# Graph network with residual norms: three buffers of dst rows, preloaded groups spread over the first pass, convolutions in halves

## What is computed

```python
N, E, D, H, L = 50000, 12500, 256, 8, 3       # nodes, edges sorted by dst, features, heads, layers
# 1. attention over the edges, relu, residual, layer norm over all nodes
h = x @ W;  e = leaky_relu(a_src[src] + a_dst[dst], 0.2)
alpha = exp(e - segment_max(e, dst)[dst]) / (segment_sum(...)[dst] + 1e-16)
x = layernorm(x + relu(segment_sum(h[src] * alpha, dst) + bias))
# 2. three edge convolutions, each followed by a batch norm; residual, layer norm
y = x
for l in range(3):
    e = relu((y[dst] - y[src]) @ theta[l].T + y[src] @ phi[l].T)
    agg = where(segment_max(e, src) < -1e30, 0, segment_max(e, src))
    y = relu((agg - agg.mean(0)) * rsqrt(agg.var(0) + 1e-5) * gamma[l] + beta[l])
return layernorm(x + y)
```

## Time and profile before

| | us |
|---|---|
| runs (three), median and extremes | 1758.32 (1757.24 to 1765.64) |
| the profiled execution, own time | 1768.92 |
| its span | 1767.1 |
| granted TensorE clock, mean of the span | 0.834 |
| PE busy | 1076.6 |
| DVE busy | 1239.4 |
| ACT busy | 985.7 |
| POOL busy | 955.6 |

### The profile page before, as it was taken

The page is one execution under the profiler, slowest core; times in us unless marked ns, Lnnn a source line. Parts: engine busy times, 40 slices in busy tenths (PEclk is TensorE's granted clock), DMA queues, the critical chain, the costliest instruction groups (busy, mean ns, idle before and its releaser), DMA issues.

```text
span 1767.1 us, 16600 instructions
## 1 busy us (share of the span) xinstructions
PE 1076.6 (61%) x3823; PEld 562.5 (32%) x3823; DVE 1239.4 (70%) x2657; ACT 985.7 (56%) x2630; POOL 955.6 (54%) x1013
## 2 busy tenths in 40 slices
PE   0139888781004661699999699997999987000000
PEld 0023333330002331455555355554545544000000
DVE  8847877678978994255455355563666678989998
ACT  4735877665455775244444455564555453766665
POOL 1047756667767777777777677524544137640000
PEclk9999999895557876799999899998999999555555
DMA  9276899988694674588886589856866359999999
GB/s 366 101 227 214 284 324 354 334 306 257 222 294 157 202 228 144 155 261 264 255 269 203 120 187 202 184 162 122 153 141 134 84 186 309 420 412 389 383 404 366
DMA packets 174965, 431.98 MB, mean 244 GB/s; under 512 B 28308, under 2 KB 107682, under 8 KB 154900
## 3 DMA queue, kind: packets, MB, share of 16 engines
q1 hardware_dynamic: 107748, 227.24, 37.0%
q0 software_dynamic: 43904, 98.91, 22.9%
q10 hardware_dynamic: 23216, 104.77, 16.8%
HBM read 254.11 MB, written 180.72 MB: 246 GB/s over the span
## 4 chain that ended last, share of the span: by engine, by line
PE 42%; DMA 20%; DVE 20%; issue 6%; POOL 5%; ACT 4%; SPq 2%; ACTq 0%; POOLq 0%; DVEq 0%
PE ps L1296 14%; PE ps L1309 14%; DMA out<-arena 10%; PE ps L1286 4%; DMA arena<-x 3%; DMA x_dst<-arena 3%; DVE stat L806 2%; PE ps L1473 2%; PE ps L1325 2%; PE ps L887 2%; DMA arena<-x,idx 2%; POOL x L1162 2%; ACT arena L845 2%; DVE arena L1068 2%; DVE arena L803 2%
## 5 line engine op out<-in xcount | busy, mean ns | idle before, releaser
L1381 DVE TENSOR_TENSOR_SCAN arena<-arena,ps 128x512 f32<-128x512 f32 (+1 forms) x150 | 186.7, 1253 | 242.5 <-PE ps L1296 209.2
L860 POOL DMA_INDIRECT arena<-x,idx x196 | 186.1, 949 | 182.5 <-DVE idx L622 90.8
L1267 POOL DMA_INDIRECT arena<-agg,slot x196 | 185.3, 945 | 181.4 <-PE ps L1286 80.4
L1309 PE MATMUL ps<-arena 128*128 128x512 f32 x600 | 269.5, 592 | 10.5 <-ACT arena L1351 10.5
L1296 PE MATMUL ps<-arena 128*128 128x512 f32 x600 | 270.1, 593 | 0.0
L1242 POOL DMA_INDIRECT arena<-x,idx x196 | 185.6, 947 | 61.0 <-issue 57.0
L1578 ACT ACTIVATE ps<-arena 128x256 f32<-128x256 f32 x391 | 143.7, 367 | 96.4 <-DVE arena L1550 96.4
L845 ACT ACTIVATE arena<-arena,shift,inv 128x256 f32<-128x256 f32 (+1 forms) x311 | 156.1, 589 | 50.9 <-DVE shift L837 34.2
L1385 DVE TENSOR_TENSOR ps<-arena,ps 128x512 f32<-128x512 f32 (+1 forms) x150 | 101.7, 683 | 96.6 <-PE ps L1309 96.3
L1351 ACT ACTIVATE arena<-big,bn_shift,bn_scale 128x512 f32<-128x512 f32 (+1 forms) x100 | 75.1, 798 | 162.1 <-PE ps L1309 150.3
L1309 PEld LDWEIGHTS ps<-arena 128*128 128x128 f32 x600 | 115.5, 193 | 151.5 <-issue 139.9
(11 more groups left out here) (214 smaller groups left out, 2166.9 us busy)
## 6 DMA issues: line engine op xcount, KB each, us to landing
arena<-x SPq DMA_DIRECT2D x39, 1280.0 KB, 9.3
out<-arena SPq DMA_DIRECT2D x39, 1280.0 KB, 11.8
arena<-x ACTq DMA_DIRECT2D x31, 1280.0 KB, 10.5
x<-arena ACTq DMA_DIRECT2D x31, 1280.0 KB, 6.4
agg<-arena SPq DMA_DIRECT2D x48, 512.0 KB, 4.1
arena<-not_same SPq DMA_DIRECT2D x72, 256.0 KB
arena<-last_of SPq DMA_DIRECT2D x72, 256.0 KB
x_dst<-arena SPq DMA_DIRECT2D x24, 512.0 KB, 3.6
```

The costliest lines, as they stand in the source:

```text
L860: pl.indirect_dma_start(rows_in[:, par, a, g, :], None, x[:, :], bass.IndirectOffsetOnAxis(ap=idx[:, k, t * G + g:t * G + g + 1], axis=0)) ...
L1267: pl.indirect_dma_start(conv_in[:, b, 1, g, :], None, agg_dram[l - 1][:, :], bass.IndirectOffsetOnAxis(ap=slot[:, t * G + g:t * G + g + 1] ...
L1309: m = pe.matmul(near_bank[j][:, 0:width(t)], thp[:, l, 1, k, j * P:(j + 1) * P], near_t[:, par, k, 0:width(t)], start=(k == 0), stop=(k == 1))
L1381: v.tensor_tensor_scan(runmax[:, par, j, 0:width(t)], mask[:, tl % 2, 0:width(t)], far_bank[j][:, 0:width(t)], initial, ALU.add, ALU.max). ...
```

## The change

1. **Third buffer of dst rows** (`rows_dst_3`, `DST_RING`). The buffers of dst rows go round by three, with three semaphores each for gathered and stored. POOL waits for the store of tile t-3, and for the transposes of that tile's dst rows only, before the dst gathers of tile t; the wait for the transposes of tile t-2 stands before the src gathers. The space comes from `msq` and `tiles_f`, which now lie in `score`.
2. **Preloaded groups spread.** The eight groups in `big` are those of the steps 0, 3, 5, 8, 11, 13, 15 and 18 of the first pass and no longer of the steps 0 to 7. `pre_node_rows` says which nodes a group now has.
3. **Convolution 0 by halves.** PE takes the far transposes of tile t, the near product of tile t-1, the near transposes of t, the rows of t-2, the far product of t. ACT copies rows two steps behind and not three, ahead of the squares.
4. **Starts of convolutions 1 and 2.** PE makes the far product of tile 0 before the transposes of tile 1. Before and after the near product of tile 0 stand four and five products whose result nothing reads (`keep_clock`).
5. **SP** loads masks ahead of the store of rows in a step, and at the end the stores come before the last mask load. ACT copies the last rows ahead of the last squares.

```diff
-        s_dst_got = [sem("dst_got_0"), sem("dst_got_1")]
+        DST_RING = 3
+        s_dst_got = [sem(f"dst_got_{b}") for b in range(DST_RING)]
...
-        s_xd_stored = [sem("xd_stored_0"), sem("xd_stored_1")]
+        s_xd_stored = [sem(f"xd_stored_{b}") for b in range(DST_RING)]
...
+        rows_dst_3 = sb("rows_dst_3", [P, G, D])
...
-        score = sb("score", [H, 2, SUP])
+        score = sb("score", [P, 2, SUP])
...
-        msq = sb("msq", [P, DENSE_RING, PR])
+        msq = score[:, 0, 0:DENSE_RING * PR].rearrange("p (b r) -> p b r", r=PR)
...
-        tiles_f = sb("tiles_f", [1, PG + 1])
+        tiles_f = score[0:1, 1, 0:PG + 1]
...
+        BIG_STEPS = (0, 3, 5, 8, 11, 13, 15, 18)
+        BIG_GROUPS = [PRE_SORT + k for k in BIG_STEPS]
+        RING_GROUPS = [g for g in range(PG + 1) if g not in BIG_GROUPS]
+        assert len(BIG_STEPS) == PRE_BIG
+
         def in_big(g):
 
-            return PRE_SORT <= g < PRE_SORT + PRE_BIG
+            return g in BIG_GROUPS
 
         def ring_use(g):
 
-            return g if g < PRE_SORT else g - PRE_BIG
+            return RING_GROUPS.index(g)
 
         def group_at(use):
 
-            return use if use < PRE_SORT else use + PRE_BIG
+            return RING_GROUPS[use]
+
+        def pre_node_rows(g):
+            if in_big(g):
+                return node_rows(PRE_SORT + BIG_GROUPS.index(g))
+            return node_rows(g if g < PRE_SORT else PRE_BIG + ring_use(g))
 
         RING_USES = PG + 1 - PRE_BIG
 
         def pre_rows(g):
             if in_big(g):
-                lo = NS * 2 * SUP - (PRE_SORT + PRE_BIG - g) * PR * D
+                lo = NS * 2 * SUP - (PRE_BIG - BIG_GROUPS.index(g)) * PR * D
                 return big[:, lo:lo + PR * D].rearrange("p (r f) -> p r f", r=PR)
             return pre[:, ring_use(g) % PRE_RING, :, :]
...
 
         def loaded(e, g):
             if in_big(g):
-                e.wait_ge(s_big_x[(g - PRE_SORT) * 2 // PRE_BIG], 16)
+                e.wait_ge(s_big_x[BIG_GROUPS.index(g) * 2 // PRE_BIG], 16)
             else:
                 e.wait_ge(s_rows_in[ring_use(g) % PRE_RING], 16 * (ring_use(g) // PRE_RING + 1))
 
...
 
         def pre_load(a, use):
             g = group_at(use)
-            rows, p, r = node_rows(g)
+            rows, p, r = pre_node_rows(g)
             b, u = use % PRE_RING, use // PRE_RING
             if u:
                 a.wait_ge(s_rows_stored[b], 16 * u)
...
+
+        def dst_rows(t):
+            b = t % DST_RING
+            return rows_dst_3 if b == 2 else rows_in[:, b, 1, :, :]
+
+        def src_rows(t):
+            return rows_in[:, t % 2, 0, :, :]
+
         def gat_pool(pl):
             pl.wait_ge(s_idx, 3)
             pl.wait_ge(s_first_turned, 1)
             for t in range(NS):
-                par = t % 2
+                if t >= DST_RING:
+                    pl.wait_ge(s_row_turned, 4 * (t - DST_RING) + 2)
+                    pl.wait_ge(s_xd_stored[t % DST_RING], 16 * (t // DST_RING))
+                for g in range(cols(t)):
+                    pl.indirect_dma_start(dst_rows(t)[:, g, :], None, x[:, :],
+                                          bass.IndirectOffsetOnAxis(ap=idx[:, D_DST, t * G + g:t * G + g + 1], axis=0)).then_inc(s_dst_got[t % DST_RING], 16)
                 if t > 1:
                     pl.wait_ge(s_row_turned, 4 * (t - 1))
-                    pl.wait_ge(s_xd_stored[par], 16 * (t // 2))
-                for a, k, got in ((1, D_DST, s_dst_got), (0, D_SRC, s_src_got)):
-                    for g in range(cols(t)):
-                        pl.indirect_dma_start(rows_in[:, par, a, g, :], None, x[:, :],
-                                              bass.IndirectOffsetOnAxis(ap=idx[:, k, t * G + g:t * G + g + 1], axis=0)).then_inc(got[par], 16)
+                for g in range(cols(t)):
+                    pl.indirect_dma_start(src_rows(t)[:, g, :], None, x[:, :],
+                                          bass.IndirectOffsetOnAxis(ap=idx[:, D_SRC, t * G + g:t * G + g + 1], axis=0)).then_inc(s_src_got[t % 2], 16)
 
...
-                    if j == 0:
-                        pe.wait_ge((s_src_got, s_dst_got)[a][t % 2], 16 * cols_landed(t, 2))
+                    if n == 0:
+                        pe.wait_ge(s_dst_got[t % DST_RING], 16 * cols_landed(t, DST_RING))
+                    if n == 2:
+                        pe.wait_ge(s_src_got[t % 2], 16 * cols_landed(t, 2))
+                    rows = dst_rows(t) if a else src_rows(t)
                     if t:
                         pe.wait_ge(s_row_kept, 4 * (t - 1) + n + 1)
...
-            sp.wait_ge(s_dst_got[t % 2], 16 * cols_landed(t, 2))
-            sp.dma_start(xd_dram[edges(t), :].rearrange("(g p) f -> p g f", p=P), rows_in[:, t % 2, 1, 0:cols(t), :]).then_inc(s_xd_stored[t % 2], 16)
+            sp.wait_ge(s_dst_got[t % DST_RING], 16 * cols_landed(t, DST_RING))
+            sp.dma_start(xd_dram[edges(t), :].rearrange("(g p) f -> p g f", p=P), dst_rows(t)[:, 0:cols(t), :]).then_inc(s_xd_stored[t % DST_RING], 16)
...
             def store(t):
                 sp.wait_ge(s_agg_kept, banks_before(l, t) + row_banks(t))
                 sp.dma_start(agg_dram[l][edges(t), :].rearrange("(g p) f -> p g f", p=P), agg_rows[:, t % 2, 0:cols(t), :]).then_inc(s_agg_stored[t % 2], 16)
-            first = 2 if l else 0
-            for s in range(first, NS + 3):
-                if l < L - 1 and 0 <= s - 3:
-                    store(s - 3)
-                if s < (NS + 2 if l < L - 1 else NS):
-                    masks(s)
+            lag = 2 if l == 0 else 3
+            for s in range(2 if l else 0, NS):
+                masks(s)
+                if l < L - 1 and s >= lag:
+                    store(s - lag)
             if l < L - 1:
+                masks(NS)
+                for t in range(NS - lag, NS):
+                    store(t)
+                masks(NS + 1)
                 for par in range(2):
                     sp.wait_ge(s_agg_stored[par], 16 * tiles_before(par, l + 1, 0))
                 sp.sem_inc(s_agg_ready, 1)
...
-            def turn(t):
+            def turn(t, near_rows):
                 b = t % RC
-                pe.wait_ge(s_far_got[b], 16 * far_landed(l, t))
-                for n in range(4 if l == 0 else 2):
+                if near_rows:
+                    pe.wait_ge(s_near_got[b], 16 * cols_landed(t, RC))
+                else:
+                    pe.wait_ge(s_far_got[b], 16 * far_landed(l, t))
+                for n in (2, 3) if near_rows else (0, 1):
                     a, j = 1 - n // 2, n % 2
-                    if n == 2:
-                        pe.wait_ge(s_near_got[b], 16 * cols_landed(t, RC))
...
+            def keep_clock(count):
+                pe.wait_ge(s_conv_scan, 2 * NS * l)
+                for _ in range(count):
+                    pe.matmul(far_bank[0], ident[:, :], thp[:, l, 0, :, :].rearrange("p k f -> p (k f)"), start=True, stop=True)
 
...
-            if l:
-                near(0)
-            in_steps([(0, turn), (1, products)] + ([(2, rows)] if l < L - 1 else []), NS)
+            if l == 0:
+                for t in range(NS):
+                    turn(t, False)
+                    if t > 0:
+                        near(t - 1)
+                    turn(t, True)
+                    if t > 1:
+                        rows(t - 2)
+                    far(t)
+                near(NS - 1)
+                rows(NS - 2)
+                rows(NS - 1)
+                return
+            keep_clock(4)
+            near(0)
+            keep_clock(5)
+            turn(0, False)
+            far(0)
+            turn(1, False)
+            far(1)
+            near(1)
+            for s in range(2, NS + 2):
+                if s < NS:
+                    turn(s, False)
+                if 2 < s <= NS:
+                    far(s - 1)
+                    near(s - 1)
+                if l < L - 1:
+                    rows(s - 2)
...
-            in_steps([(0, keep)] + ([(3, keep_rows)] if l < L - 1 else []) + [(2, squares)], NS)
+            for s in range(NS + 2):
+                if s < NS:
+                    keep(s)
+                if l == 0 and s >= 2:
+                    keep_rows(s - 2)
+                if l == 1 and s >= 3:
+                    keep_rows(s - 3)
+                if l == 1 and s == NS + 1:
+                    keep_rows(NS - 1)
+                if s >= 2:
+                    squares(s - 2)
```

34 lines of the change are left out of this document (15 added, 19 removed).

## The result

The changed kernel takes 1751.05 us, the median of 13 runs (1740.52 to 1756.00), against 1767.12 us for 13 runs of the kernel before (1756.40 to 1777.27). The ratio is 0.991, with a 95% interval of 0.988 to 0.993. So the change is faster by 0.9%, where the prediction had 2.0% and 1723.0 us (1702 to 1744). About a third of the miss in microseconds is the base: the three runs of before that the prediction started from had a median of 1758.3 us, the 13 runs 1767.1. The rest, and all of the miss in the ratio, is gain that did not come. The profiled execution has a span of 1745.9 us (own time 1747.75), before 1767.1.

A forecast was written before the change was run, and what follows sets the result against it. It took POOL as near full in almost every stage and as convolution 0's bound. Terms 20.2 + 3.2 + 4.9 + 2.0 + 5.2 = 35.5 us off 1768.9 gave 1733.4, ratio 0.980; from median 1758.3, 1723.0 us (1702 to 1744).

The forecast's parts named there:

- First pass: Tile 24's score 20.2 us earlier (bounds 6 and 28): store waits gone, 10.6 us a step, earlier start.
- ACT with PE: First pass: 10.25 us a step from the light stretch, one of three nearly equal limits beside POOL 10.01 and DMA 10.26.
- the start: First pass: tile 2's gathers wait 5.95 us for a store queued behind SP's loads; 5.1 us of it gained.
- Tail of the puts: End of message stage: POOL is later than the data today, DVE's path becomes the later; 3.2 us more (0 to 3.2).
- Cap between convolutions 0 and 1: PE ends convolution 0 twelve us early, but POOL's twenty look-ups cap the gain at 4.9 us (0 to 6).
- Start of convolution 1: Far product of tile 0 before tile 1's turn gains 2.0 us (0 to 2.6); tile 3's rows may hold part back.
- Start of convolution 2: Gain 5.2 us (1 to 6): store of last sums 0.9 us sooner, PE's start to tile 2's turn 4.4 shorter.
- PE stays busy through the extra products: Start of convolution 2: PE busy up to the first turn at first gather G + 8.1, product in 3.44 us, not 4.73.
- 0.3 us in the way: Start of convolution 2: near half plus five products end about G + 8.4 (G: first gather), costing 0.3 us.
- DMA stays the bound: Rival, first pass: store waits become later landings, only the start's 6 us gained; total 21.3 us, 1737 us, chance 0.22.
- the pass's gain is given back behind it: Rival: pass's gain lost between its end and 541 us, convolutions' 12 us or less stay; 1750 to 1758 us, chance 0.09.
- ACT would wait for stores ahead of loads: Rival, first pass: ACT's loads wait for stores, delaying copies PE needs; slower, 1767 us, chance 0.05.

The follow-up runs named there:

- the stalled chip: Kernel before took 2105 us there; first runs, against it: convolutions' order alone 0.996, changed kernel with two dst buffers 1.001, without spread 0.988, with late square root 0.981.
- the run without a pause: Changed kernel with other extra-product counts around tile 0's near product: 8 and 9 in convolution 1, 9 and 2 in convolution 2; 1746.1 us, ratio 0.989.

## Why the prediction was wrong

**First pass (20.2 predicted, 12.2 came).** The waits for stores did go, as said (35.2 to 4.3 us), and the third buffer was needed for it. The step that failed is the price of 10.6 us a step; it measured 10.84. I read the light stretch's 10.25 us as a limit of "ACT with PE" that would stay, and set a mean between it and the heavy stretch. It was a loop of two tiles, which the kernel before showed too, in its scores of the light stretch (start, us):

```profile
185.97 0.68 DVE L920 COPY score<-ps 8x512 f32<-8x512 f32 x1 [3.17 <-PE ps L887]
194.88 0.68 DVE L920 COPY score<-ps 8x512 f32<-8x512 f32 x1 [0.49 <-PE ps L887]
206.48 0.68 DVE L920 COPY score<-ps 8x512 f32<-8x512 f32 x1 [3.18 <-PE ps L887]
```

They stand 8.91 and 11.60 us apart by turns, 20.51 a pair. Every full tile is the same work, so one full engine would give steps of one length; a loop of two tiles can give two. Read as a loop, the effect of the spread could have been priced in part: a round's load adds 0.47 us (20.98 against 20.51), which is 10.49 us a tile at the full clock and still inside the 10.6. What took the pass beyond it is the clock, which had no term in the sum: the pause on PE grows from 2.39 to 2.88 us, and the clock falls behind most of these pauses. The light stretch went from 10.25 to some 11.5 us a step (171.78 to 217.75 is 46.0 us for four), and gave back part of what the heavy stretch won. The other 2.4 us are the start. Half of it is that I let tile 1 follow tile 0 after 7.7 us, but PE needs 8.8 for a tile, and it took 8.8 in every run but those on the stalled chip and those with two buffers. The other half is tile 0's own score, at 131.88 and not 130.65; it lies between 130.0 and 132.7 in the other runs off the stalled chip.

**Tail of the puts (3.2, 1.6).** The mechanism was right: POOL reached the puts 20.9 us earlier and had to wait for data. The size was off because POOL was not empty when tile 22 was ready: its last real wait for data (1.81 us) ended at 665.98, with 18 puts to go, not ten, and 18 puts of 1.28 us end at 689.0.

**Cap between convolutions 0 and 1 (4.9, 5.9).** Right in mechanism, and near in size: the first gather now waits for the last look-up, 2.12 us, and not for the store. Convolution 0 itself stayed at POOL's 10.0 us a tile, as said.

**Start of convolution 1 (2.0, 1.7).** Right for this execution, including that tile 3's rows hold back part of it. It was partly luck: in three other executions with this order the same point came 0.9 to 2.4 us later than the 37.2 of the kernel before. The extra products were hidden, as said; they were also useless.

**Start of convolution 2 (5.2, 0.0).** The gather did start earlier after PE's last transpose of sums (5.1 us after it, before 6.6: 1.4, predicted 0.9). Two steps failed. I said that "PE stays busy through the extra products", so that the near half runs in 3.44 us; in fact four products end 4.5 us too early, since the wait for a store ahead of the squares (2.08 us on ACT) put the statistics later than I had counted, by about two and a half us and not one. The near half ran at half the clock, and the "0.3 us in the way" became 5.3. Second, I ended the count at the turn of tile 2 (G + 23.8). The order puts the turn of tile 3 ahead of the products of tile 2, and its rows are not there before G + 26.3: with everything else as predicted (the run without a pause: turn of tile 2 at G + 22.9) the near half of tile 2 ends 1.7 us earlier than before, not 4.4.

**Rivals.** That DMA stays the bound came nearest in the ratio (21.3 us of 1768.9 are 0.988, measured 0.991), but it was not the cause: leaving out three quarters of the dst stores gave DMA 0.09 of its share back and the pass did not move. The measured 1751 us lie in the range of another rival, that the pass's gain is given back behind it (1750 to 1758), and that is luck of the base: nothing was given back, the 12.2 us at the last score were 13.9 at the first gather of convolution 0. That ACT would wait for stores ahead of loads was not seen. The rival that was missing is the one that held for the pass: a loop through three engines, none of them full.

## What to carry over

Steps that alternate between two lengths can point to a loop over two buffers or two groups; follow the chain once around it before giving an engine or DMA the blame, and look in it for an instruction that waits early for something needed late. What the loop issues counts, DMA issues of 0.4 us too, because the engine that pauses may come back at half its clock. Extra work that is to hold a clock has to reach up to the next real work without a pause, and must not stand ahead of it; if a transfer bounds the stage anyway, leave it out. And a count of a stage's start ends at the first wait that the new order puts ahead of the products, not at the one that it removed.
